# Cross-attention with an image prompt, one core: three of the first tile's five x pieces issued by ScalarE, and three places where the load queue waits for a landing

## The reference, cut to what matters

```python
q = split_heads(x @ w_q, 20)                    # x: (2, 2048, 640), 20 heads of 32
k = split_heads(text @ w_k, 20)                 # text: (2, 69, 1024)
v = split_heads(text @ w_v, 20)
out_text = merge(softmax(q k^T / sqrt(32)) v)
k_ip, v_ip = image_tokens @ w_k_ip, image_tokens @ w_v_ip     # 8 image tokens
out_ip = merge(softmax(q k_ip^T / sqrt(32) + mask_from_boxes) v_ip)
out = (out_text + out_ip) @ w_out + b_out + x
```

## Time and profile before

| | |
|---|---|
| median of 3 runs | 400.89 us (400.56 to 401.34) |
| profiled execution, its own time | 403.38 us |
| profiled execution, span from first to last instruction | 401.6 us |
| granted TensorE clock, mean of the span | 0.999 of full speed |
| bytes moved by DMA in the span | 72.96 MB |

### The profile page before, as it was taken

How to read it: one execution, slowest core, us unless ns; L and a number is a source line. 1 busy time by engine, 2 the same in 40 slices (tenths; PEclk the granted TensorE clock), 3 DMA queues, 4 the chain that set the end, 5 groups by cost and what they waited for, 6 DMA issues and landing times.

```text
span 401.6 us, 10790 instructions
## 1 busy us (share of the span) xinstructions
PE 392.8 (98%) x4452; PEld 291.1 (72%) x4452; DVE 339.1 (84%) x459; ACT 129.7 (32%) x196; POOL 154.2 (38%) x127
## 2 busy tenths in 40 slices
PE   8989999999999999999999999999999999999996
PEld 6778777767777777677777776777777767776775
DVE  4588669989999998899999998998999989989623
ACT  5244333445324322352234322342323322223100
POOL 0057522378526423374226433363226442222200
PEclk9999999999999999999999999999999999999999
DMA  8899926487547544674458445664447554455565
GB/s 285 327 356 365 241 76 176 147 232 217 161 142 230 166 123 128 196 230 130 141 138 257 124 120 155 208 189 138 141 138 247 138 145 125 125 137 147 141 189 194
DMA packets 42993, 72.96 MB, mean 182 GB/s; under 512 B 10560, under 2 KB 10688, under 8 KB 42944
## 3 DMA queue, kind: packets, MB, share of 16 engines
q1 hardware_dynamic: 37824, 67.02, 54.5%
q10 hardware_dynamic: 5120, 5.25, 5.2%
HBM read 35.53 MB, written 10.49 MB: 115 GB/s over the span
## 4 chain that ended last, share of the span: by engine, by line
PE 85%; DMA 5%; DVE 4%; POOL 2%; ACT 1%; SPq 1%; issue 1%; DVEq 0%
PE ps L646 66%; PE ps L695 9%; PE ps L681 8%; DMA stage<-in_x 3%; PE ps L734 2%; DMA x_raw<-in_x 1%; DMA stage<-in_w_out 1%; POOL prob L359 1%; SPq L242 1%; DVE den L530 1%; ACT prob L397 1%; DVE text_max L506 1%; DVE prob L512 1%; DVE prob L523 1%; DVE prob_t L542 0%
## 5 line engine op out<-in xcount | busy, mean ns | idle before, releaser
L359 POOL TENSOR_TENSOR prob<-prob,rden 128x1104 f32<-128x1104 f32 x40 | 82.2, 2055 | 199.0 <-DVE rden L535 199.0
L542 DVE STREAM_TRANSPOSE prob_t<-prob 128x1536 f32<-128x1536 f32 x40 | 70.7, 1767 | 0.1
L397 ACT ACTIVATE prob<-prob 128x1232 f32<-128x1232 f32 x40 | 50.0, 1250 | 59.0 <-DVE prob L523 59.0
L506 DVE TENSOR_REDUCE text_max<-ps 128x16 f32<-128x1104 f32 x40 | 52.2, 1304 | 18.0 <-PE ps L681 17.6
L646 PE MATMUL ps<-x_hi,wq_hi 128*128 128x512 f32 x200 | 59.0, 418 | 1.3 <-ACT q L393 0.7
L646 PEld LDWEIGHTS ps<-x_hi,wq_hi 128*128 128x128 f32 x200 | 34.6, 188 | 34.8 <-issue 27.7
L440 ACT ACTIVATE o_hi<-ps 128x512 fp32r<-128x512 f32 x40 | 23.7, 592 | 101.9 <-PE ps L695 98.1
L646 PE MATMUL ps<-o_hi,wo_hi 128*128 128x512 f32 x200 | 55.8, 392 | 0.6 <-ACT o_hi L440 0.6
L646 PE MATMUL ps<-o_hi,wo_lo 128*128 128x512 f32 x200 | 55.1, 389 | 0.0
L646 PE MATMUL ps<-o_lo,wo_hi 128*128 128x512 f32 x200 | 55.1, 389 | 0.0
L530 DVE TENSOR_REDUCE den<-prob 128x16 f32<-128x1104 f32 x40 | 50.6, 1264 | 4.9 <-ACT prob L397 4.9
(11 more groups left out here) (58 smaller groups left out, 341.3 us busy)
## 6 DMA issues: line engine op xcount, KB each, us to landing
prob_k<-prob_t SPq DMA_DIRECT2D x320, 64.0 KB
stage<-in_x SPq DMA_DIRECT2D x40, 256.0 KB, 3.2
res<-in_x SPq DMA_DIRECT2D x35, 256.0 KB
out_tiles<-res SPq DMA_DIRECT2D x35, 256.0 KB, 2.3
prob_k<-prob_t ACTq DMA_DIRECT2D x160, 32.0 KB
wki_raw<-in_w_k_ip SPq DMA_DIRECT2D x5, 512.0 KB, 7.6
wv_raw<-in_w_v SPq DMA_DIRECT2D x5, 512.0 KB, 8.3
wvi_raw<-in_w_v_ip SPq DMA_DIRECT2D x5, 512.0 KB, 10.3
```

The costliest lines, as they stand in the source:

```text
L359: nc.gpsimd.tensor_tensor(e[:, :, 0:TEXT], e[:, :, 0:TEXT], rden[:, par, 0, :].unsqueeze(2).to_broadcast([P, QT * HG, TEXT]), ALU.mult)
L397: nc.scalar.activation(prob[:, c % 2, :, 0:TOKENS], prob[:, c % 2, :, 0:TOKENS], ACT.Exp).then_inc(exp_done, 1)
L506: nc.vector.tensor_reduce(text_max[:, par, :, :], s[:, :, :, 0:TEXT], AX_X, ALU.max).then_inc(text_max_done, 1)
L542: nc.vector.transpose(prob_t[:, c % 2, :, :, :].rearrange("p k n r -> p n k r"), prob[:, c % 2, :, :].rearrange("p n (k r) -> p n k r", r= ...
```

## The change

ScalarE issues the first tile's x pieces 0, 2 and 4 at the head of its list; SP keeps pieces 1 and 3. SP gets three waits: behind x piece 3, until piece 0 has landed; ahead of the grid, until piece 4 has landed; and ahead of the first image-value weights (`wvi` piece 0), until image-key weights 3 (`wki` piece 3, the second load into its slot, hence the 32) have landed. The order of the loads in the second half of the prologue is changed too.

```diff
             def prologue():
                 load(("w_q", 0))
-                for kt in range(KD):
+                for kt in range(1, KD, 2):
                     sp.dma_start(x0_raw[:, kt, :], x[kt]).then_inc(x0_loaded[kt], 16)
+                sp.wait_ge(x0_loaded[0], 16)
                 load(("w_q", 1))
...
+                sp.wait_ge(x0_loaded[4], 16)
                 sp.dma_start(grid_sb[:, :], grid).then_inc(grid_loaded, 16)
...
                 load(("w_q", 2))
                 load_k(2, wk_raw, w_k, wk_loaded)
                 load_k(2, wki_raw, w_k_ip, wki_loaded)
+                load_v(0, wv_raw, w_v, wv_loaded)
                 load(("w_q", 3))
-                load_v(0, wv_raw, w_v, wv_loaded)
+                load_k(3, wk_raw, w_k, wk_loaded)
+                load_k(3, wki_raw, w_k_ip, wki_loaded)
+                sp.wait_ge(wki_loaded[1], 32)
                 load_v(0, wvi_raw, w_v_ip, wvi_loaded)
                 load(("w_q", 4))
-                load_k(3, wk_raw, w_k, wk_loaded)
-                load_k(3, wki_raw, w_k_ip, wki_loaded)
                 load_v(1, wv_raw, w_v, wv_loaded)
                 load_v(1, wvi_raw, w_v_ip, wvi_loaded)
...
             def prologue():
+                for kt in range(0, KD, 2):
+                    act.dma_start(x0_raw[:, kt, :], x[kt]).then_inc(x0_loaded[kt], 16)
                 high(("w_q", 0))
```

## The result

The changed kernel took 407.53 us (median of 6 runs, 407.47 to 408.63), the kernel before 400.73 in the same comparison (6 runs, 399.33 to 401.34): a ratio of 1.0179, 95% interval 1.0159 to 1.0199. It is 6.8 us slower. The forecast had the sign and the place, and a quarter of the size (1.6 us); the time lies above its range (399.8 to 404.2) and above the high end of its own sum (4.4 us more, 405.3).

The account below looks back on a forecast made before the run. PE, busy 392.8 of 401.6 us, was taken as the bound, with start-up set by the load queue until x piece 9 lands. That landing 1.6 us later, start gain included, gave 400.89 + 1.6 = 402.5 us, range 399.8 to 404.2.

Parts of the forecast that it names:

- the high end of its own sum: Start gain 0 and load landings of 6.2 and 5.0 us: x piece 9 at 53.0, or +4.4 us.
- the wait for key weights 3 goes: Prologue, PE: key weights 3 found landed at 26.6, the 1.4 us wait gone, PE 2.0 us early to v_fold(0).
- the gaps near 22 and 28 us: Load queue: DMA shares well under 1 before key weights 3 are issued and again at the hold.
- X piece 9 was foreseen at 50.2: End of start-up: x piece 9 lands 1.6 us later than 48.58, putting v_fold(1) at 51.2 instead of 49.63.
- Where the early PE goes: At v_fold(0): ScalarE through at 38.2, v_fold(0) about 38.6, PE's 2.0 us spent waiting; v_fold(1) at 51.2.
- The start: First x pieces on two issuers: copy_q(0) starts at 10.07, not 10.64, 0.6 us gained (bounds 0 and 1.4).
- the start gives nothing: Rival for the x pieces: everything 0.6 later, 403.1 us, up to 405.3 with slow restarts; chance 0.13.
- The hold: SP ahead of image-value weights 0: image-key weights 3 land after 5.2 us at 28.7, image-value weights 0 after 3.8 at 32.5.
- The 2.16 MB behind them: Loads from image-value weights 0 (32.5) through x piece 7, landing at about 37.6: 5.1 us.
- an emptied queue gives time back: Load queue: 1.5 us given back because no DMA engine lags behind the others; called the least certain part.
- The fast rival: Load queue: emptying it twice removes the lag, x piece 9 lands before 47.8, about 399.7 us; chance 0.2.
- No change: Rival: holds are cheap, start gives 1.4, pair lands in 4.7, wvi 0 in 3.5; 400.9 us; chance 0.22.

Follow-up runs that it names:

- e14: Changed kernel plus 20 filling matmuls on TensorE just ahead of v_fold(0), in its wait: 406.48 us, ratio 1.0129 to the kernel before.
- e3: Kernel before with only ScalarE issuing x pieces 0, 2 and 4 and the holds on x pieces 0 and 4: 401.07 us, ratio 1.0009.
- e1: Changed kernel without the hold on image-key weights 3, new load order kept: 402.35 us, ratio 1.0049 to the kernel before.
- e2: Kernel before with only the new order of loads and the hold on image-key weights 3: 407.49 us, ratio 1.0173.
- e13: Changed kernel as it is, timed again beside e14: 408.29 us, ratio 1.0169 to the kernel before.
- e8: Kernel before with hi and lo of x pieces 5 to 7 and 8 to 9 made one step later: 403.67 us, ratio 1.0082.
- e11: Kernel before with ScalarE's part of e8, GpSimd making lo of x pieces 8 and 9 in its old place: 399.79 us, ratio 0.9969.
- e10: Changed kernel, SP's hold waiting for key weights 3 in place of image-key weights 3: 405.61 us, ratio 1.0127 to the kernel before.
- e7: Changed kernel with hi and lo of x pieces 5 to 7 and 8 to 9 made one step later: 404.39 us, ratio 1.0099 to the kernel before.
- e12: Changed kernel with the same late places for hi and lo as e11: 405.49 us, ratio 1.0116 to the kernel before.

## Why the prediction was right in sign and wrong in size

**Held:** that the holds put idle time on the queue and that PE pays for it in a fold; that PE comes early to v_fold(0) and waits there, since copy_v_part(0) stands behind x pieces 5 to 7; that the wait for key weights 3 goes; the gaps near 22 and 28 us. X piece 9 was foreseen at 50.2: in e14, the same loads with the clock kept up, it landed at 50.4. That number is in part luck: in e14 x piece 7, on the way there, came at 40.1 and not at 37.6.

**Failed: the step "Where the early PE goes".** It put ScalarE's end at 38.2 and v_fold(0) at 38.6; it was 41.84, and no wait was left at v_fold(1), on which the whole sum had been made. Four terms in it or ahead of it were wrong; the third and the fourth weigh most.

1. *The start: 0.6 us, measured 0.* The x pieces landed 4.1 to 5.8 us after their issue, and not within 3.5. copy_q(0) did start sooner (10.31, foreseen 10.07, before 10.64). But the hold behind x piece 3 had SP issue image-key weights 0 at 5.74, which landed at 13.03, where the kernel before had them at 12.3, and PE waited for them (the 0.3 us of the first fence). I had costed the later issues at nothing because the x pieces would cover them; the stretch of 7 to 8 us, at a share of 0.75 (before: 0.97), is where that cover was gone. So key weights 3 were issued at 23.73, before at 23.68. (Such times move between executions: e3, with the same first half, issues them at 23.40.) The rival "the start gives nothing" had this right. w_q piece 0 landed at 4.7, 0.8 us later than before (wq_hi starts at 4.73, in the earlier trace rows at 3.93). The Trainium skill (DMA: Bandwidth & Descriptors, "Queues, rings and completion order") says that a DMA engine takes the queues that have work for it in turn, packet by packet. The trace agrees in that both queues move at once: from 1 to 3.9 us SP's has 0.31 MB and ScalarE's 0.21, where before SP's had 0.64 alone. The sum is smaller by 0.12 MB, so sharing is not all of the delay, and the turns themselves no row shows.
2. *The hold: 5.2 us to the landing of image-key weights 3, measured 5.8; then 3.8 for image-value weights 0, measured 3.4.* With the start, image-value weights 0 landed at 33.3, foreseen 32.5.
3. *The 2.16 MB behind them: 5.1 us, measured 7.4* (33.3 to 40.8). I took the rate of a queue that runs full (2.16 MB in 5.1 us are 423 GB/s, where the earlier trace rows had 393); in e1, without the hold, it was 5.2 us, as assumed (30.9 to 36.1). Behind the hold the engines are as busy, but move less. First the changed kernel, then e1 (columns as above):

```profile
33.00:38.00 5.00, 3.34 (x34) 2.48 (x33) 4.93 (x6) 0.74 (x1) 3.95 (x3) 1.00 0.98 349
```

```profile
31.00:36.00 5.00, 5.00 (x118) 4.15 (x110) 4.89 (x9) 2.11 (x4) 3.00 (x3) 1.00 1.04 408
```

   349 GB/s against 408; e2, e13 and e14, with the same hold, have 373, 350 and 371 in 33 to 38 us. Why is open. From 33.3 to 40.8 it is 344: at 408 GB/s the same 2.16 MB would take 5.3 us, at 344 they take 6.3, so the lower rate makes some 1.0 us of the 2.3 (an estimate). The rest is other bytes among them: 344 GB/s over 7.5 us are 2.6 MB. Part of these are the four moves of ScalarE, whose packets before began to go behind 36 us, when x pieces 5 to 7 had landed, and which now share the engines with those pieces. In 38 to 42 us it is (DMA queues: packets, MB, share)

```profile
q1 hardware_dynamic: 425, 1.20, 93.3%
q10 hardware_dynamic: 128, 0.13, 11.5%
```

   with all 128 packets of those moves in it (q10 is ScalarE's queue), and x pieces 5, 6 and 7 landing 1 us apart. That an emptied queue gives time back was true of single loads (3.4 to 3.6 us instead of 6.65), and false of the stretch.
4. *The clock: not in the sum at all.* Foreseen was an idle stretch of some 2 us; at 5.5 us the granted clock fell, which costs 1.8 us (e13 against e14).

Together: v_fold(0) 3.8 us later, and the half clock behind it, less the 1.0 us that PE no longer waits in v_fold(1), is 3.8 + 1.6 - 1.0 = 4.4, which is what the trace has for v_fold(1) (53.98 against 49.63, less rounding), 1.6 being 12.1 us from fold to fold in the changed kernel less 10.5 in e14. The span ends 4.1 later.

**The other 2.7 us come, most likely, from the profile that the forecast started from.** The 2.0 us that PE was to come early rest on a wait of 1.43 us for key weights 3 in the earlier trace rows. Three more traces have the old order of loads, and hardly show it: e3, e8 and e11. In e3 and e11 these weights landed 4.7 and 4.9 us after their issue (6.65 in the kernel before), and PE did not wait; in e8 it waited for 0.3 us. e3:

```profile
28.52 2.04 PE L738 MATMUL ps<-ctx_sb,wk_raw 128*128 128x138 f32 x16
...
35.94 0.40 PE L780 MATMUL ps<-eye_sb,img_part 128*128 128x16 f32 x2
...
48.04 0.40 PE L780 MATMUL ps<-eye_sb,img_part 128*128 128x16 f32 x2 [1.49 <-ACT img_part L418]
```

PE takes key weights 3 at 28.52 and not at 30.38, and v_fold(0) comes at 35.94 (36.06 in e8, 35.89 in e11) and not at 38.05. Against e3 the changed kernel is 5.9 us late at v_fold(0) and 5.9 at v_fold(1), and its span is 5.2 longer, with e3's profiled execution still 1.3 us above its median. So the profiled execution of the kernel before stood where it did, 2.5 us above the median, most likely by this late load. I took the 2.5 us off to get to the median, and left in the sum the gain that only such an execution can have. No second trace of the kernel before itself was taken to see it directly.

**The fast rival** ("the lag goes with the depth") fell: its loads did land in 3.5 us, but x piece 7 came later, not sooner. **No change** fell too, by e2.

## What to carry to other kernels

A wait put into the list of the engine that issues the loads stops everything behind it: ask what stands there and who wants it, and count the landing (here 5.8 us, in the last two of which the queue stood at a share of 0.06), not the issue. Before costing a delay, look at how long an idle stretch it makes on TensorE; a long one (3.0 us in e10, not the 1.5 of e3) is charged twice, once as the wait and once as the half clock behind it. Before building a forecast on a wait of one profiled execution that is slower than the median, see whether another execution has it. And a wait that looks like a late load may be an engine's own order: the better place for the copies was worth 1.2 us to the kernel before, where the first half of the change was worth nothing.

## What was not expected of the hardware

- An idle stretch of TensorE of 3.0 us (e10) took the granted clock to 0.50, and so did one of 2.9 (e1, in its second wait). Waits of 1.0 to 1.5 us left it at 1.00; of those of 1.8 and 1.9 it stayed up in e7 and e12 and fell in e8. In e8 and e1 it fell only when PE was at work again, 1.0 to 1.5 us behind the end of the wait. In e10 it was low until past 44 us, in the changed kernel until past 45, with PE fully at work since 38.7 and 41.8.
- A load of 512 KB on an empty queue landed after 3.4 to 3.9 us and the second of a pair after 5.5 to 5.9, while 4.7 had been read from one pair of the kernel before.
- Behind the hold the DMA engines moved 349 to 373 GB/s at a share near 1 for 5 us (33 to 38 us, four traces), where 408 had gone at that share without it (e1).
- Executions of one kernel differ by up to 5.6 us (25 runs of the kernel before: 399.3 to 404.9), the two slowest of them with a lower mean clock, where the changed kernel's six first runs, all at 0.990 to 0.992, lie within 1.2 us.
